# Another order of steps in a software-pipelined two-layer graph attention kernel

## The reference

```python
x = layernorm(x + L0(x, adj));  x = layernorm(x + L1(x, adj))
# L0
alpha = softmax(relu((x @ wq) @ (x @ wk).T) * (adj != 0), axis=1)
out = alpha @ (x @ weight)
# L1, 16 heads of 32
scores = where(adj == 0, -inf, q @ k.T / sqrt(32));  out = softmax(scores) @ v @ Wo + bo
```

## Time and profile before

| | |
|---|---|
| median of 3 runs | 2682.06 us (2681.98 to 2684.6) |
| the profiled execution's own time | 2676.25 us |
| its span in the trace | 2674.5 us |
| busy share of PE, DVE, ACT, POOL | 94%, 83%, 74%, 29% |
| granted TensorE clock, mean | 0.981 of full speed |

### The profile page before, as it was taken

The page is one execution under the profiler, slowest core; times in us unless marked ns, Lnnn a source line. Parts: engine busy times, 40 slices in busy tenths (PEclk is TensorE's granted clock), DMA queues, the critical chain, the costliest instruction groups (busy, mean ns, idle before and its releaser), DMA issues.

```text
span 2674.5 us, 66209 instructions
## 1 busy us (share of the span) xinstructions
PE 2501.8 (94%) x24648; PEld 1328.5 (50%) x24648; DVE 2217.6 (83%) x4052; ACT 1984.5 (74%) x6286; POOL 773.5 (29%) x1416
## 2 busy tenths in 40 slices
PE   6899999999999999999999999999999999999995
PEld 3444555455555445555445555445555445555442
DVE  4588888888888888888888888888888888888885
ACT  3477777777777777877777777777877777777775
POOL 0123322333331233331333331333331233321332
PEclk9999999999999999999999999999999999999997
DMA  4266656666656666656666656666655676656655
GB/s 151 69 118 123 127 104 128 130 133 125 131 106 127 123 138 126 124 106 122 129 133 127 129 106 125 125 136 128 127 107 126 121 135 124 125 108 126 127 99 108
DMA packets 1023090, 326.55 MB, mean 122 GB/s; under 512 B 969904, under 2 KB 986288, under 8 KB 1022768
## 3 DMA queue, kind: packets, MB, share of 16 engines
q1 hardware_dynamic: 1022768, 322.32, 60.6%
HBM read 49.55 MB, written 33.55 MB: 31 GB/s over the span
## 4 chain that ended last, share of the span: by engine, by line
PE 70%; DVE 12%; DMA 8%; issue 4%; POOL 3%; ACT 3%; SPq 1%; DVEq 0%; POOLq 0%; ACTq 0%
PE front L330 62%; DMA pT<-p_p 5%; PE pv_bank L330 4%; DVE sm L633 3%; PE s_bank L419 3%; DVE p_p L533 2%; DMA oT<-o_p 1%; DVE nmax L637 1%; DVE z_sb L658 1%; POOL y_p L690 1%; POOL ln L684 1%; ACT e L512 1%; DMA yT<-y_p 1%; DVE ln L661 1%; DVE ln L616 1%
## 5 line engine op out<-in xcount | busy, mean ns | idle before, releaser
L512 ACT ACTIVATE e<-sm,nmax 128x128 f32<-128x128 f32 x2048 | 790.9, 389 | 85.1 <-DVE nmax L637 67.5
L693 POOL TENSOR_TENSOR o_p<-o_sb,o_p 128x512 f16<-128x512 f32 x128 | 153.1, 1196 | 998.4 <-ACT o_p L525 998.4
L330 PE MATMUL front<-W_O,oT 128*128 128x512 f16 x1536 | 379.8, 400 | 54.0 <-DMA oT<-o_p 54.0
L533 DVE SCALAR_TENSOR_TENSOR p_p<-e,p_p 128x512 f16<-128x512 f32 x512 | 390.9, 764 | 28.3 <-ACT p_p L520 24.2
L512 ACT ACTIVATION_READ_ACCUMULATOR e<-sm,nmax 128x1 f32 x2048 | 385.9, 188 | 0.0
L330 PE MATMUL front<-yT,W_K 128*128 128x512 f16 x1536 | 350.0, 381 | 26.3 <-DMA yT<-y_p 26.2
L637 DVE TENSOR_REDUCE nmax<-sm 128x4 f32<-128x512 f32 x512 | 351.2, 686 | 17.7
L633 DVE SCALAR_TENSOR_TENSOR sm<-s_bank,maskb 128x512 f32<-128x512 f32 x512 | 348.7, 681 | 10.2 <-PE s_bank L419 9.9
L330 PE MATMUL front<-xT,W_A 128*128 128x512 f16 x1536 | 344.2, 381 | 9.7 <-DMA xT<-x_p 9.7
L330 PE MATMUL front<-yT,W_Q 128*128 128x512 f16 x1536 | 352.3, 379 | 0.0
L330 PE MATMUL front<-W_V,yT 128*128 128x512 f16 x1536 | 352.3, 379 | 0.0
(11 more groups left out here) (90 smaller groups left out, 3247.6 us busy)
## 6 DMA issues: line engine op xcount, KB each, us to landing
x_sb<-in_x SPq DMA_DIRECT2D x128, 256.0 KB, 3.6
out_x<-z_sb SPq DMA_DIRECT2D x128, 256.0 KB, 2.5
adj_i<-in_adj SPq DMA_DIRECT2D x32, 256.0 KB, 4.9
pT<-p_p SPq DMA_TRANSPOSE x512, 3.1
xT<-x_p SPq DMA_TRANSPOSE x128, 2.7
yT<-y_p SPq DMA_TRANSPOSE x128, 2.7
oT<-o_p SPq DMA_TRANSPOSE x128, 3.2
y_sb<-in_L_gnn_wq SPq DMA_DIRECT2D x1, 1024.0 KB, 5.6
```

Source lines behind the costliest of these rows:

```text
L330: mm = pe.matmul(bank, left(a), right(b), start=(k == 0 and n == 0), stop=(k == of - 1 and n == 2))
L512: act.activation(e1[:, k % 2, h, :], sm[:, count(g, STEPS, k) % SM_BUFS, h, :], ACT.Exp, bias=nmax[:, count(g, STEPS, k) % SM_BUFS, h:h + ...
L533: return dve.scalar_tensor_tensor(out=dst, in0=src, scalar=scale, in1=hi, op0=ALU.mult, op1=ALU.subtract)
L693: pool.tensor_tensor(o_p[:, LO, :], o_sb[:, :], o_p[:, HI, :], ALU.subtract).then_inc(olo_ready, 1)
```

## The change

`PASS` is replaced by another list with the same 161 steps. Operations, buffers, waits and semaphores are the same, only the order in which each engine comes to its steps changes, and with it the ages of some steps (`t` 0 and 1, `adj01` and `adjT` of the next group now stand at the end of a pass, `q` and `k` 2 and 3, `v(0)` and `S(0)` stand in their own group's pass). The list is cyclic, so that an age that changes by one together with a move across the list's start is no move at all.

```diff
 PASS = [
-    ("q", 2, 1), ("P", 14, 2), ("x_parts", 2, 0), ("k", 2, 1), ("exp", 15, 2), ("o", 2, 2), ("k", 3, 1), ("x_parts", 3, 0),
...
+    ("S", 1, 1), ("sm", 4, 1), ("sm", 5, 1), ("exp", 3, 1), ("pT", 0, 1), ("P", 2, 1), ("oT", 2, 2), ("t", 2, 0), ("P", 3, 1),
...
```

More of the change, by code:

```diff
@@ L58 @@
 PASS = [
[21 rows of a table removed]
[10 rows of a table added]
+    ("oT", 1, 1), ("exp", 9, 1), ("y_parts", 2, 0), ("norm0", 3, 0), ("y_parts", 3, 0), ("mask_size", 0, 0), ("yT", 2, 0),
[10 rows of a table added]
 ]
```

## The result

| | before | changed |
|---|---|---|
| median of 6 runs | 2682.02 us (2678.2 to 2684.6) | 2706.62 us (2696.54 to 2711.17) |
| ratio, with its 95% interval | | 1.0086 (1.0070 to 1.0102) |
| span of the profiled execution | 2674.5 us | 2694.7 us |
| granted clock, mean | 0.981 | 0.976 |

The account below looks back on a forecast made before the run. PE's waits, mostly hanging on the end of the last g, were taken to bound the kernel; +18.6 us for the load and −2 us for the drain gave +16.6 us, some 2698 us, range of 8 in 10 2664 to 2720.

Parts of the forecast that it names:

- The cluster behind the last g costs nothing: PE from the last g to the first projection: S(3) waits more, fin(1) less; cost 0, 0.1 us either side.
- The load ahead of pT(9) is the price: SP's queue: the load follows yT(3) at once, pT(9) lands behind it, so PE waits at PV(9); +0.62 us a pass.
- The size of that price: PE's wait at PV(9): between 1.0 and 3.2 us, taken as 1.1, in place of 0.48 us a pass at PV(10).
- +18.6 us for the thirty passes: Cost of the load's new place: 1.1 − 0.48 = +0.62 us for a pass, times 30.
- The clock: Rival: fin(1) slow in every pass, 21 more at 1.7 us each, 36 us, giving 2734; chance 0.07.
- The count of slow fin(1) far from nine: One of three signs of a wrong prediction; nine of thirty fin(1) took 4.45 us where others took 2.76.
- The rest of the pass costs nothing: z block, S(1), oT(3) and others: costed at nothing, with margins of 0.4 to 1 us.
- The drain, −2 us: End of the kernel: norm1(2) no longer ahead of P(5), saving 2 us, between −5 and +3.
- The rate of the Trainium skill: Some 358 GB/s from HBM: load takes 3.7 us, pT(9) lands about load + 6.4, so no wait.
- The four waits of the earlier trace: PE's waits before the change, read as 113 us over the span, nearly all in the steady part.

Follow-up runs that it names:

- e1: The changed kernel with the load moved behind pT(9), as in the kernel before; 2662.48 us, ratio 0.9935.
- e2: The kernel before with the load moved ahead of pT(9), the store still ahead of both; 2731.07 us, ratio 1.0180.
- e4: The changed kernel with four additional 128x512 matmuls in the pause ahead of fin(1); 2694.11 us, ratio 1.0058.
- e11: The changed kernel with the load behind pT(11) and four additional matmuls ahead of fin(1); 2649.48 us, ratio 0.9887.
- e8: The kernel before with norm1(2) moved behind P(8), as in the new order; 2680.61 us, ratio 1.0007.
- e7: The kernel before with the load right behind yT(3), ahead of the store and of pT(9); 2749.25 us, ratio 1.0261.
- e10: The kernel before with the load moved behind pT(11) and nothing else; 2676.78 us, ratio 0.9984.
- e12: The kernel before with the last graph's store (norm1(3)) ahead of yT(0), yT(1) and oT(1) moved behind it; 2675.65 us, ratio 0.9983.
- e5: The changed kernel with the load moved behind pT(11); 2660.17 us, ratio 0.9932.
- e9: The kernel before with the last graph's store (norm1(3)) moved behind pT(11); 2852.08 us, ratio 1.0648.
- e6: The changed kernel without the loads of x for all groups but the first, adjacency still loaded; 2647.39 us, ratio 0.9881.

## Why the prediction was right, point by point

The forecast was 2698 us, the result is 2706.6; +16.6 us was worked out, +24.6 came, and +20.2 between the two profiled executions, to which the steps are held.

- **The cluster behind the last g costs nothing.** Right in its sum: the first projection starts 6.29 us behind S(3) in place of 6.20. S(3) waits 1.05 us and not 1.21 only because the forecast took the spacing of two jobs (2.59) for the length of one (2.75); it starts 3.80 us behind the last g's end, as forecast. But the equality is not the chain's. The last yT is issued 0.4 us earlier (2.50 us behind S(3) against 2.92, means of thirty passes), since POOL is free earlier than the forecast had it, and in the pass shown the wait for yT is 0.35 us and not 0.8. (fin(1) waits 0.86, forecast 0.9.) The slow fin(1) take that back: where fin(1) isn't slow the first projection starts 5.66 us behind S(3) in place of 5.81, but 15 passes have a slow one in place of ten.
- **The load ahead of pT(9) is the price.** Right, and shown from both sides: e1 takes the step back and the loss is gone, e2 makes it alone in the old order and loses 50 us, and e4 against e11 shows it where no fin(1) is slow.
- **The size of that price was luck in part.** Forecast: PV(9) 6.3 us behind the first projection; measured 6.35. Two terms behind it were off by about 1 us each, and they cancel. The forecast let pT(9) land 9.0 us behind Y, the issue of the last yT, with 7.7 us from the load's start; that was near the shortest of the thirty passes before (7.4), whose mean was 8.4. Measured, it landed 9.9 us behind Y. And it let the first projection start at Y + 2.76 in every pass; measured, that is Y + 3.8 (Y + 3.3 before), because a slow or late fin(1) often comes between. With the mean landing of the kernel before in the same sum the thirty passes would have come to (1.3 + 8.4 − 7.96 − 0.48) × 30 = 38 us in place of 18.6. The wait itself is 0.92 us a pass; 0.24 us more of the delay shows as slower jobs ahead of it.
- **+18.6 us for the thirty passes.** Measured 22.0. The 3.4 us more are small pieces: +2.6 up to the first projection, +1.9 from there to PV(9), +1.2 behind PV(9) to S(0), −2.2 in the rest. Slow jobs have a part in them: five q and k are slow that weren't before, three of them behind a pause at PV(9), as at 580.41 above, at some 1.7 us each. The clock stood as a rival and was put at nothing in the sum.
- **The count of slow fin(1) far from nine** was to make the prediction wrong. It went to 15 and did not, since they are mostly hidden (e4). In the kernel before it was ten and not nine: one more stands at 1446.23 (4.45 us). A count of slow jobs isn't a cost.
- **The rest of the pass costs nothing.** Right: 49.00 against 49.07 us, and no wait for the z block, S(1) or alpha.
- **The drain, −2 us.** It gave 3.0, but for another reason than mine (e8), so this term was right by luck. All six kernels in the new order with the loads take 102.9 to 106.0 us from the last full S(3), the six old ones with a free z_sb buffer (before, e2, e7, e8, e10, e12) 106.5 to 108.1. What makes the difference is open.
- **The rate of the Trainium skill** (page "DMA: Bandwidth & Descriptors", section "Where 436 GB/s comes from") would have hidden the load, by the estimate of 6.4 us from its start to pT(9). The trace has 8.5 us in the mean, so the rows were the better guide.
- **Two readings of the rows were off without a consequence.** The four waits of the earlier trace rows add up to 132.6 us and not 113; 99 us of them lie in the thirty passes. And of the 18 waits for pT 17 are at PV(10), the eighteenth (0.19 us) is elsewhere.
- The median grew by 4 us more than the profiled executions did; the profiled one of the changed kernel, 2696.54 us, is the fastest of its six.

**Open.** With the load in the same place the new order is 0.5% faster than the old (e5 against e10, e1 against before). In the traces of e5 and e10 the gain is 0.57 us a pass: 0.29 up to the first projection, where e5 issues the last yT 0.29 us earlier and has four slow fin(1) fewer, 0.08 from PV(9) to S(0), where e5 waits less for a bank, 0.20 in the rest, nearly all of it the waits for pT that e10 has and e5 hasn't; and 3.4 us in the drain. No run separates these pieces by an edit of its own.

## What to carry to other kernels

A bulk load that nobody waits for can still be the most expensive step of a queue: what it costs is decided by who stands behind it, and here its exchange of places with one transpose was worth some 40 us in the new order (e1) and 50 us in the old (e2). Before a reordering is costed by engine, list for each DMA queue the first transfer behind every bulk transfer, and compare its landing (start of the bulk transfer to landing, from the trace) with the moment at which its reader comes. Take that landing from all passes and not from one (here 7.4 to 9.9 us, mean 8.4). Ask of a transfer that is moved back which buffer it frees (e9). And where a slow clock and a wait share a stretch, take the slow jobs out of both kernels before comparing (e4 against e11): PE's totals alone would have put the loss on the clock.

## What the runs showed of the hardware

The clock of PE fell in this kernel with pauses far shorter than a pass. Windows of the changed kernel, with PE's busy time, its instructions and the granted clock behind POOL's column: a slow fin(1), one that isn't, and the projection behind the pause at PV(9).

```profile
327.90:332.40 4.50, 4.45 (x13) 1.71 (x14) 4.40 (x9) 3.69 (x17) 2.14 (x5) 0.62 0.82 205
...
569.70:572.50 2.80, 2.76 (x12) 1.09 (x12) 2.73 (x6) 2.02 (x9) 1.07 (x3) 1.00 0.82 184
...
580.40:584.80 4.40, 4.40 (x24) 1.69 (x21) 2.04 (x2) 0.64 (x3) 3.36 (x4) 0.61 0.60 114
```

The first has 0.62, between the levels of 1.2 and 2.4 GHz, the second full speed behind nearly the same pauses (1.05 and 0.86 us, against 1.05 and 0.89); the third 0.61 behind two projections at full speed and a pause of 1.90 us. So nearly the same pauses do and don't bring the clock down, and I could tell from these rows only a share of slow jobs: 4 of 30 (e6) to 21 of 30 (e7) fin(1) over these kernels, and none with four more matmuls in the pause (e4, e11). This agrees with what the Trainium skill says in "TensorE: Matmul & The Clock Gate", section "Loop structure matters more than you think", that matmuls kept together keep the clock up.

In the kernel before a DMA transpose of y or x takes 2.7 us from issue to landing (medians). A pT of the same size took 5.8 us behind 1.3 MB of loads, counted from its own issue (mean of thirty passes, 4.6 to 7.0), and a store of 256 KB between the two made its landing some 1.0 us later (e7). From the start of the load to the landing of the first pT behind it the mean is 8.2 to 8.6 us in all eleven kernels that load x and have nothing between the two, whether that pT is 9, 10 or 12.
